# Moving bulk loads, late weight loads and semaphore credits to later places in the first tiles of a fused two-layer kernel

## What is computed

```python
x = x + tanh(g_xattn[0]) * L0_xattn(layernorm(x), ctx, w_qkv, w_proj, b_proj)   # 16 heads of 8
x = x + tanh(g_ffn[0])   * L0_ffn(layernorm(x), gate_w, sh_*, rt_*)             # top-1 of 8 experts, and a shared one
x = x + tanh(g_xattn[1]) * L1_xattn(layernorm(x), ctx, mask, W_in, ...)         # depooled context
x = x + tanh(g_ffn[1])   * L1_ffn(layernorm(x), router_w, expert_w, ...)        # top-2 of 8 experts
```

## Time and profile before

| | us |
|---|---|
| median of three runs | 494.19 |
| lowest and highest run | 491.52, 498.88 |
| span of the profiled execution | 490.0 |
| PE busy | 443.7 (91%) |
| DVE busy | 366.8 (75%) |
| POOL busy | 319.4 (65%) |
| ACT busy | 277.8 (57%) |

### The profile page before, as it was taken

The page is one execution under the profiler, slowest core; times in us unless marked ns, Lnnn a source line. Parts: engine busy times, 40 slices in busy tenths (PEclk is TensorE's granted clock), DMA queues, the critical chain, the costliest instruction groups (busy, mean ns, idle before and its releaser), DMA issues. The chain is left out here.

```text
span 490.0 us, 20510 instructions
## 1 busy us (share of the span) xinstructions
PE 443.7 (91%) x6871; PEld 349.2 (71%) x6872; DVE 366.8 (75%) x1201; ACT 277.8 (57%) x775; POOL 319.4 (65%) x780
## 2 busy tenths in 40 slices
PE   5789999989999999997987999987997799899998
PEld 3456677756766666774666988864655799898997
DVE  3668999978898989944768666545766678788984
ACT  2468899877988888764234545434233434444431
POOL 3845765567777777767723666577825899898630
PEclk9889999998999999989999999998999699999999
DMA  7941231111111110100245776631000011111001
GB/s 232 413 152 41 48 36 27 26 31 40 28 32 33 30 36 22 37 20 18 76 131 158 228 227 216 222 121 37 18 5 13 16 46 33 46 37 37 23 23 33
DMA packets 37394, 37.38 MB, mean 76 GB/s; under 512 B 20440, under 2 KB 31504, under 8 KB 36816
## 3 DMA queue, kind: packets, MB, share of 16 engines
q0 software_dynamic: 7552, 20.20, 12.9%
q1 hardware_dynamic: 29200, 16.06, 11.9%
q10 hardware_dynamic: 576, 0.26, 0.2%
HBM read 24.82 MB, written 7.86 MB: 67 GB/s over the span
## 5 line engine op out<-in xcount | busy, mean ns | idle before, releaser
L979 DVE TENSOR_REDUCE negm<-PS 128x4 f16<-128x512 f32 x128 | 81.9, 681 | 0.4
L716 ACT ACTIVATE pexp<-PS 128x512 f32<-128x512 f32 x128 | 69.4, 595 | 6.4 <-PE PS L1383 5.8
L1725 PE MATMUL PS<-w,vp 128*128 128x128 f32 x512 | 63.3, 277 | 0.0
L1725 PEld LDWEIGHTS PS<-w,vp 128*128 128x128 f32 x512 | 60.6, 194 | 0.0
L1396 PEld LDWEIGHTS PS<-pexp,vp 128*32 128x32 f32 x2048 | 34.5, 113 | 26.4 <-issue 20.5
L1396 PE MATMUL PS<-pexp,vp 128*32 128x64 f32 x2048 | 50.3, 230 | 0.3
L1619 PE MATMUL PS<-xsT,wst 128*128 128x128 f32 x320 | 44.4, 282 | 3.0 <-DVE stack L1217 1.3
L1619 PEld LDWEIGHTS PS<-xsT,wst 128*128 128x128 f32 x320 | 38.8, 191 | 7.3 <-issue 5.0
L581 POOL DMA_INDIRECT sorted_x<-VALL,posu x32 | 33.3, 1040 | 13.4 <-issue 7.6
L611 POOL DMA_DIRECT2D wst<-in_rt_gate_up_dram x40 | 21.5, 538 | 29.2 <-PE PS L1619 19.9
L1310 DVE TENSOR_TENSOR vp<-PS,xnT 128x1024 f32<-128x1024 f32 x32 | 38.6, 1205 | 0.8 <-PE PS L1702 0.8
(11 more groups left out here) (246 smaller groups left out, 1254.5 us busy)
## 6 DMA issues: line engine op xcount, KB each, us to landing
wst<-in_rt_gate_up_dram POOLq DMA_DIRECT2D x40, 256.0 KB, 3.5
xs<-sorted_x SPq DMA_DIRECT2D x40, 64.0 KB, 2.8
sorted_y<-YS POOLq DMA_DIRECT2D x40, 64.0 KB, 3.0
out_dram<-X SPq DMA_DIRECT2D x32, 64.0 KB
X<-in_x_dram SPq DMA_DIRECT2D x1, 1536.0 KB, 8.2
CK<-in_ctx_k_dram SPq DMA_DIRECT2D x1, 1536.0 KB, 12.2
CV<-in_ctx_v_swapped_dram SPq DMA_DIRECT2D x1, 1536.0 KB, 16.6
rdn<-in_rt_down_dram POOLq DMA_DIRECT2D x1, 1024.0 KB, 10.6
```

The costliest lines, as they stand in the source:

```text
L716: nc.scalar.activation(pexp[:, j, :], PS[:, 2 + j % 2, :], ACT.Exp).then_inc(S["exped"], 1)
L979: dve.tensor_reduce(negm[:, a.par, :, j], PS[:, j % 2, :].rearrange("p (g k) -> p g k", g=G), AX.X, ALU.max, negate=True).then_inc(S["maxe ...
L1725: nc.tensor.matmul(PS[:, 6 + y.par, 0:D], z[:, y.par, e, :], w1[:, e * D:e * D + D], start=(e == 0), stop=False)
```

## The change

Three moves; no instruction is added or removed, apart from where it stands.

1. **Bulk loads.** The 1536 KB parts of X, CK and CV and `shgu` leave SP's opening list. SP issues each right behind a shift transfer: X's behind that of tile 0, CK's behind tile 1's, CV's behind tile 2's, `shgu` behind tile 3's.
2. **Late loads.** POOL issues its 18 late loads at tiles 8 to 16 and not at tiles 2 to 10, the zeros transfer with the first of them.
3. **Credits.** 16 of DVE's 31 credits move behind its work for tile 2 (7), tile 3 (5) and tile 5 (4).

```diff
-            for c in range(3):
+            for c in range(2):
                 lo, hi = TILE_CHUNKS[c]
...
-            for dst, src in ((shgu, sh_gate_up),):
-                sp.dma_start(dst[:], src).then_inc(more_in, 16)
+
+            def load_behind(n):
+
+                lo, hi = TILE_CHUNKS[2]
+                if n < 3:
+                    dst, src = ((X, x), (CK, ctx_k), (CV, ctx_v_swapped))[n]
+                    sp.dma_start(dst[:, lo * D:hi * D], src[:, lo * D:hi * D]).then_inc(rest_in, 16)
+                elif n == 3:
+                    sp.dma_start(shgu[:], sh_gate_up).then_inc(more_in, 16)
...
                     sp.dma_start(qc[24:P:32, a.slot, :, :], mT[:, a.par, :]).then_inc(shift_placed[a.par], 16)
+                    if a.turn is None and a.n < 4:
+                        load_behind(a.n)
...
-                if l and 2 <= l.n < 11:
-                    for dst, src in late_loads[2 * l.n - 4:2 * l.n - 2]:
+                if l and 8 <= l.n < 17:
+                    for dst, src in late_loads[2 * l.n - 16:2 * l.n - 14]:
                         pool.dma_start(dst[:], src).then_inc(late_in, 16)
-                    if l.n == 2:
+                    if l.n == 8:
                         pool.dma_start(sorted_x[E * REGION:ROWS].rearrange("(p r) d -> p (r d)", p=P), zeros[:])\
                             .then_inc(spare_zero, 16)
...
-            credit(dve, ("h_acted", 2), ("h_added", 1), ("e_acted", 1), ("e_kept", 1),
-                   *((n, 1) for n in ("c_dp_kept c_picked c_put l_stats l_moments l_x3 l_stats2 l_moments2 "
-                                      "l_masked l_out_ready").split()), ("l_choice", 4))
-            dve.sem_inc(sq_summed, 2)
+
+            def later_credits(n):
+                if n == 2:
+                    credit(dve, ("h_acted", 2), ("h_added", 1), ("e_acted", 1), ("e_kept", 1),
+                           *((n, 1) for n in "c_dp_kept c_picked c_put".split()))
+                elif n == 3:
+                    credit(dve, *((n, 1) for n in "l_stats l_moments l_x3 l_stats2 l_moments2".split()))
+                elif n == 5:
+                    credit(dve, ("l_masked", 1), ("l_out_ready", 1), ("l_choice", 4))
+                    dve.sem_inc(sq_summed, 2)
...
+                if l and l.turn is None:
+                    later_credits(l.n)
```

More of the change, by code:

```diff
@@ L898, in _ @@
             quad_credit(dve, ("k_choice", 5), ("k_placed", 2))
-            credit(dve, ("h_acted", 2), ("h_added", 1), ("e_acted", 1), ("e_kept", 1),
-                   *((n, 1) for n in ("c_dp_kept c_picked c_put l_stats l_moments l_x3 l_stats2 l_moments2 "
-                                      "l_masked l_out_ready").split()), ("l_choice", 4))
-            dve.sem_inc(sq_summed, 2)
+            def later_credits(n):
+                if n == 2:
+                    credit(dve, ("h_acted", 2), ("h_added", 1), ("e_acted", 1), ("e_kept", 1),
+                           *((n, 1) for n in ("c_dp_kept c_picked c_put".split())))
+                elif n == 3:
[3 more added lines that the diff above has]
+                    dve.sem_inc(sq_summed, 2)
             dve.memset(stack[:, 1], 0.0).then_inc(odd_stack, 1)
```

## The result

The changed kernel is slower. Its median is 500.78 us over four runs (495.87 to 502.84); the kernel before, run beside it, has 496.31 us over four (491.52 to 498.88). The ratio is 1.018, with a 95% interval of 1.012 to 1.024: the direction is clear of the noise, and whether it is more than 2% is not. The forecast was 492.1 us, with a range up to 497.0. The two profiled executions are 11.3 us apart (span 501.3 against 490.0): that of before is the fastest of its four and that of after the slowest, so they lie at the upper end of the 6 to 12 us that the interval stands for.

A forecast was written before the change was run, and what follows sets the result against it. PE, busy 91% of the span, was taken as the bound, with something to win at the walk's start. -1.58 + 0.6 - 0.14 - 0.95 = -2.07 us took the median 494.19 to 492.1 us, range 489.1 to 497.0.

The forecast's parts named there:

- the shift wait: PE's wait for tile 0's shift transfer behind the idle products: would go whole, gaining 1.58 us.
- nothing gained: Late loads leaving the early steps: POOL did not set the pace there, so no gain.
- the clock fall behind that wait: Step behind tile 0's shift wait: most of the clock fall goes too, gaining 0.95 us (0 to 1.85).
- the credits: Credits moved into DVE's stream delay the maxima PE awaits behind tiles 2 and 3: cost 0.6 us.
- the rival that had 0.25: Each credit costs its 0.10 us in DVE's stream and the clock still falls: 493.7 us, chance 0.25.
- The start: DVE starts 1.6 us earlier without 16 credits, but idle products end at 6.94: gain 0.14 us.
- X, CK and CV in time: Bulk parts issued behind the shifts land before they are needed, CV by 45.1 against 47.90: cost 0.
- POOL's issues: Issuing late loads at tiles 8 to 16 fits POOL's idle time: cost 0, tile 16 allowed 0 to 1.1 us.
- What SP issues is moved past other things: Bulk loads in SP's queue behind the shifts delay neither DVE nor the transpose behind CV: cost 0.
- late loads at a cost of 0: Late loads arriving at tiles 8 to 16, where POOL has room: taken to cost 0.
- the second rival: Step of tile 8: shift late until 1664 KB have moved, PE waits 2.0 us, 494.1 us; chance 0.10.

The follow-up runs named there:

- Part 1 alone: Only the bulk loads moved behind the shifts, late loads and credits as before, on the kernel before: ratio 1.0137 (1.0073 to 1.0201).
- part 2 alone: Only the late loads moved to tiles 8 to 16, on the kernel before: ratio 1.0036 (0.9981 to 1.0091).
- pieces from tile 4: Kernel before with late loads cut into at most 256 KB, two per step from tile 4: ratio 0.9945 (0.9892 to 0.9999).
- pieces from tile 8: Kernel before with late loads cut into at most 256 KB, two per step from tile 8: ratio 1.0053 (0.9993 to 1.0113).
- the kernel with four idle products: Pieces from tile 4 plus moved credits, with 4 instead of 14 idle products ahead of tile 0's first product: ratio to before 0.9937.
- reload: Pieces from tile 4, plus CK's 1536 KB part loaded a second time behind tile 1's shift: ratio to the kernel before 1.0054.
- reload, fewer idle products: The reload kernel with 4 instead of 14 idle products ahead of tile 0's first product; run once, time not read.
- reload in pieces: The reload kernel with the 1536 KB cut into six transfers of 256 KB issued in a row; run once, time not read.
- half: The reload kernel with only 768 KB of CK loaded again, in one transfer; run once, time not read.

## Why the prediction was wrong

**Right in size, with half of the cause: the shift wait, 1.58 us.** It went, and tile 0's score product follows the idle products. Part 1 alone showed 1.89 us at tile 4. But the prediction put the whole wait on the three bulk parts and nothing on the late loads ("nothing gained"), and part 2 alone removes it too, with 1.92 us at tile 4 (29.17). With the three parts ahead of it and no late loads the shift's last packet began at 24.38, well before PE asks for it; the 4.1 us up to 28.50 came with the burst of late loads, whose first 1664 KB make stall B where the change puts them. So the bulk loads needn't have moved for this gain. In the changed kernel itself tile 4 is only 0.24 us ahead, because the clock was at 1.2 GHz from 16.32 to 26.56 and before from 17.47 to 20.88; part 1 alone and the change run again had 3.41 us of it, and the pieces from tile 8 and the kernel with four idle products had the long fall as well, so it does not belong to the change.

**Right: the clock fall behind that wait.** The step runs at 1.00 and lasts 5.16 us, 1.24 less than before; 0.95 was forecast.

**Mis-sized, both for the better: the credits.** They were priced at 0.6 us; PE's waits on the maxima changed by +0.10 and −0.47 us in the changed kernel, and by +0.10 and −0.05 with the credits alone, beside one new wait of 0.33. That makes 0.4 us at the most, so the rival that had 0.25 falls (1.2 us). In the changed kernel PE ran at 1.2 GHz around these waits, so their being shorter there says little on the credits. The start gained 0.35 us and not 0.14: the transposition starts 0.21 us ahead of the end that the timeline gives the idle products, which I had taken for a bound.

**Right: X, CK and CV in time, and POOL's issues.** The three landed 6.5, 6.6 and 7.7 us after their issue, and DVE didn't wait at tile 8. POOL's step with three issues kept 0.61 us of idle time. Tile 16's step, the tight one, cost at most 0.7 us: the lead of before over after is 8.00 us at tile 15 and 8.66 at tile 18.

**Wrong: "What SP issues is moved past other things ... the cost is 0".** This step looked at what is queued in SP's own queue and at who needs the loaded data. It did not ask who else uses the DMA engines in that time. The instruction blocks of PE do; they stand in the list of queues on the page before, 0.6% of the 16 engines' span, and no row of the prediction names them. Before, the same bytes moved while PE had idle products and a wait ahead of it, and the block that came only at 23.50 stopped nothing. In the changed kernel they move while PE works off a block every 5 us or so. This is stall A.

The Trainium skill has the rule for it, on the page "Runtime: NRT & Kernel Launch", section "Instruction fetch mechanics": an engine's sequencer fetches its instructions in blocks of 16 KB through a DMA queue of its own, and the cost of a block boundary is mostly hidden. The first half agrees with the trace: 16 KB packets, and a stall that moved by the ten products left out. The second half doesn't hold under a large load: 0.85 to 3.06 us in seven profiles.

**Wrong: late loads at a cost of 0.** Here the mechanism was on record, as the second rival: a shift is late until the burst has moved. It put the landing at 6.3 us and the wait at 2.0, in one step; measured were 5.72 and 1.33, in one step, and 1.32 in two other profiles. The chance of 0.10 was too low: it rested on the shift standing in another queue than the loads, and that did not protect it. The rule of the Trainium skill that the prediction set beside it (page "DMA: Bandwidth & Descriptors", section on queues, rings and completion order: a semaphore's write lands only after every earlier write of that engine, across its queues) is not what held the shift here: its data packets were themselves late, the last beginning at 61.91, and the 4-byte packets behind them began from 61.90 to 62.04, while `rdn`'s still began until 62.24. Turns between the queues, which the prediction set beside that rule, fit this; why the shift's turns came so late stays open. The rival also stopped at the wait itself, "-2.07 + 2.0 = -0.1".

**Wrong for both: a stall was priced at its own length.** The prediction counted the clock fall behind the wait that goes, and none behind the waits that come. Here are PE's waits on a shift and its stops for instructions from the profiles above, with the clock fall next to each:

| stall | idle us, end | at 1.2 GHz |
|---|---|---|
| before, shift of tile 0 | 1.58, 28.83 | 31.12 to 34.53 |
| after, A and B | 2.24, 36.18; 1.33, 62.49 | 36.80 to 43.63; 64.11 to 70.94 |
| after again, A and B | 3.06, 34.97; 1.32, 60.88 | 34.98 to 41.81; 62.29 to 69.12 |
| late loads alone, B | 1.32, 55.51 | 55.65 to 62.48 |
| credits alone, shift of tile 0 | 2.19, 29.30 | 29.24 to 36.07 |
| reload, A | 1.63, 33.90 | 34.83 to 41.66 |
| reload, fewer idle products, A | 1.76, 33.27 | 33.46 to 40.29 |
| bulk loads alone | 0.85, 33.15; 2.05, 45.46 | no fall until 109.85 |
| reload in pieces; half | 0.85, 33.32; 0.87, 33.03 | no fall until 332.98; 377.03 |
| pieces from tile 8 | 0.48, 62.86; 0.64, 68.60 | no fall until 108.85 |

Nine of the ten stalls of 1.3 us and more stand next to a fall, eight of them next to one of 6.83 us; none of the five short ones does. The table leaves out one later wait of PE, on DVE's `xn`. Eight of the fourteen profiles have it between 102 and 116 us, with 1.15 to 2.18 us of idle time, and in all eight a fall began while it lasted or within 2.3 us of its end (the falls at 109.85 and 108.85 in the table are two of these). The other six have no wait over 0.65 us there, and no fall. A fall of 6.83 us at half the clock is 3.4 us of PE's work. The changed kernel's account up to tile 10 then reads: 2.24 + 1.33 for the stalls and 2 × 3.4 for the falls behind them make +10.4; −1.58 for the shift wait, −1.7 for the fall behind it and −0.35 at the start leave +6.8; the long early fall ate 1.7 of the gain (−0.24 at tile 4 instead of −1.93; this term is read off that start and not worked out), which makes +8.5. Measured: +8.14. Undoing either cause undoes its stall, and with it its fall; that the clock falls because PE stood still is argued from the table, and the 2.05 us without one speak against a fixed rule.

The table also says how far off the forecast would have been with both stalls in it: at the 4.25 us that each cost in its own comparison, −1.6 − 0.35 − 1.0 + 8.5 = +5.6 us, 499.8 us from the median of 494.19 that the prediction started from, slower by 1.1%. The range of 489.1 to 497.0 had one bound too few: the price of a late small transfer with the clock behind it.

## What to carry to other kernels

Before a large transfer is moved, list everything small that will share the DMA engines with it, the instruction blocks of every engine among them; another queue doesn't protect a small transfer. Leave large loads where the bounding engine is waiting anyway, or cut them into a few hundred KB and spread these over the steps; that gained time from tile 4 on and showed no gain from tile 8 on, and a cut issued all at once left half of the stall (0.85 of 1.63 us). And price a new stall of the bounding engine with the clock fall that may follow: 1.3 to 1.6 us of waiting cost 4.25 us a few tiles later here.

## What the hardware showed that was not expected

- PE stops in the middle of a group of equal products when its next 16 KB instruction packet is late. The profile calls it "issue" and names no semaphore. In nine of the ten such stalls told of here PE goes on 1.3 to 1.5 us after the packet's end; in the tenth, the change run again, 2.4 us after it.
- The packet's delay follows the bytes ahead of it, but not simply: 768 KB in one transfer and 1536 KB in six made the same stall, 0.87 and 0.85 us.
- The DMA engines were not short of bandwidth in the steps taken as a whole: the changed kernel moved 297 GB/s in the step before stall A, where the kernel before moved 387 GB/s in the stretch of the earlier trace rows. That points, for stall A, to the order of service and not to a lack of bandwidth; no run tests it.
- 16 increments cost about 1.5 us at DVE's start (4.12 to 2.64), 0.09 us each; in the middle of its stream they made PE's waits on the maxima longer by 0.4 us at the most (credits alone).
